# Rotary pair exchange by SBUF-to-SBUF DMAs, and small VectorE work handed to GpSimd and ScalarE, in a delta-rule attention and mixture-of-experts kernel

## The reference

```python
# attention block: 16 heads of 64
q, k, v = [silu(causal_dwconv(x @ W, cw, cb)) for W in (Wq, Wk, Wv)]     # 4 taps
q, k = rope(q), rope(k)                    # pairs (even, odd) are rotated by position
q, k = q * rsqrt(sum(q*q) + eps), k * rsqrt(sum(k*k) + eps)
beta  = sigmoid(x @ bw + bb)
alpha = exp(-exp(A_log) * softplus(x @ gkw + gkb + dt_bias))
for t in range(T):                         # delta rule, one state S per head
    o[t] = q[t] @ S + D * sum(q[t]*k[t]) * v[t]
    S = alpha[t] * (S - beta[t] * outer(k[t], k[t] @ S)) + beta[t] * outer(k[t], v[t])
on = o * rsqrt(mean(o*o) + eps) * onorm_w
y  = ((x @ Wg) * silu(on)) @ Wo
# second block: layernorm, 16 heads of 8 with softmax, then 8 experts of 512, the top 2 weighted
```

## Time and profile before

| | before |
|---|---|
| median of three runs | 5533.0 us |
| the profiled execution's own time | 5533.59 us |
| its span, first to last instruction | 5531.7 us |
| TensorE matmuls (PE) busy | 4792.2 us, 87% |
| weight loads (PEld) busy | 3609.5 us, 65% |
| VectorE (DVE) busy | 4623.1 us, 84% |
| ScalarE (ACT) busy | 3445.0 us, 62% |
| GpSimd (POOL) busy | 2085.5 us, 38% |
| mean granted TensorE clock | 0.843 of full speed |
| HBM read, written | 148.02 MB, 4.19 MB |

### The profile page before, as it was taken

The page is one execution under the profiler, slowest core; times in us unless marked ns, Lnnn a source line. Parts: engine busy times, 40 slices in busy tenths (PEclk is TensorE's granted clock), DMA queues, the critical chain, the costliest instruction groups (busy, mean ns, idle before and its releaser), DMA issues.

```text
span 5531.7 us, 111231 instructions
## 1 busy us (share of the span) xinstructions
PE 4792.2 (87%) x40448; PEld 3609.5 (65%) x40448; DVE 4623.1 (84%) x11457; ACT 3445.0 (62%) x6166; POOL 2085.5 (38%) x1485
## 2 busy tenths in 40 slices
PE   4688889988889898889898899888899888899986
PEld 2466667666667666667666677666677666677665
DVE  6888898888888888988888988888988888988852
ACT  3456666656666656766666666566666666666653
POOL 3443333443343442343443344433434433334420
PEclk7778898888888888988888888878988888888878
DMA  1001111011111011111111111111111011111011
GB/s 59 10 11 34 43 43 34 28 32 37 43 43 34 24 32 41 43 33 32 33 33 42 43 33 32 32 34 43 43 34 32 32 34 43 43 34 32 31 34 56
DMA packets 214453, 197.13 MB, mean 36 GB/s; under 512 B 13848, under 2 KB 176416, under 8 KB 209696
## 3 DMA queue, kind: packets, MB, share of 16 engines
q1 hardware_dynamic: 213920, 190.01, 11.1%
HBM read 148.02 MB, written 4.19 MB: 28 GB/s over the span
## 4 chain that ended last, share of the span: by engine, by line
DVE 52%; PE 38%; issue 8%; ACT 1%; SPq 0%; DMA 0%; POOL 0%; DVEq 0%; POOLq 0%; ACTq 0%
PE bank L984 36%; DVE acc L1390 10%; DVE tmpb L1556 6%; DVE NP L1526 6%; DVE Gam L1559 5%; DVE mx L1653 3%; DVE Gam L1512 3%; DVE moe L1738 2%; PE bank L988 2%; DVE QK L1671 1%; DVE QK L1479 1%; DVE Gam L1563 1%; DVE rot L1475 1%; DVE ms L1603 1%; DVE Kt L1543 1%
## 5 line engine op out<-in xcount | busy, mean ns | idle before, releaser
L1390 DVE SCALAR_TENSOR_TENSOR acc<-bank,conv_w,acc 128x255 f32<-128x255 f32 (+2 forms) x2304 | 925.1, 470 | 27.3 <-ACT acc L791 26.4
L717 POOL TENSOR_TENSOR sq<-acc 128x256 f32<-128x256 f32 x256 | 191.2, 747 | 1734.5 <-ACT acc L797 1722.3
L984 PE MATMUL bank<-QK 64*128 64x256 f32 (+1 forms) x4096 | 603.3, 352 | 211.8 <-DVE mx L1653 97.7
L984 PE MATMUL bank<-W,h 128*128 128x128 f32 x4096 | 579.7, 302 | 190.1 <-issue 103.3
L984 PEld LDWEIGHTS bank<-W,h 128*128 128x128 f32 x4096 | 551.7, 215 | 237.1 <-issue 129.6
L984 PE MATMUL bank<-mT,W 128*128 128x256 f32 x2048 | 626.4, 447 | 60.3 <-issue 39.7
L984 PEld LDWEIGHTS bank<-QK 64*128 64x128 f32 (+1 forms) x4096 | 288.6, 142 | 523.7 <-issue 346.0
L966 ACT ACTIVATE h<-bank,b 128x256 f32<-128x256 f32 x1024 | 416.7, 479 | 288.6 <-PE bank L984 286.7
L984 PEld LDWEIGHTS bank<-mT,W 128*128 128x128 f32 x2048 | 420.9, 220 | 219.2 <-issue 155.3
L729 POOL TENSOR_TENSOR rot<-rot,sin 128x512 f32<-128x512 f32 x256 | 337.3, 1317 | 450.8 <-DVE rot L1475 450.8
L1559 DVE TENSOR_TENSOR Gam<-Gam,tmpb 128x31 f32<-128x31 f32 (+15 forms) x992 | 448.1, 452 | 34.1
(11 more groups left out here) (226 smaller groups left out, 10275.4 us busy)
## 6 DMA issues: line engine op xcount, KB each, us to landing
W<-in_W SPq DMA_DIRECT2D x512, 256.0 KB, 3.2
QK<-QK SPq DMA_DIRECT2D x32, 1024.0 KB, 5.1
xin<-in_x SPq DMA_DIRECT2D x32, 128.0 KB, 4.7
x<-in_x SPq DMA_DIRECT2D x32, 128.0 KB, 2.1
xnG<-xnT SPq DMA_DIRECT2D x32, 128.0 KB, 1.9
out<-moe SPq DMA_DIRECT2D x32, 128.0 KB, 1.9
NP<-in_c_alpha_sel SPq DMA_DIRECT2D x1, 1024.0 KB, 5.4
Wqkv<-in_Wq SPq DMA_DIRECT2D x1, 512.0 KB, 6.1
```

What stands on the lines that cost most here:

```text
L984: return mm(out_, lhsT, rhs, start=first, stop=last)
L1390: v.scalar_tensor_tensor(acc[:, n % 2, m, j:T], ps[:, m, 0:T - j], conv_w[:, kind, c, PAD - j:KT - j], acc[:, n % 2, m, j:T], ALU.mult, AL ...
```

## The change

The result is the same function. Eight things are changed:

1. The even and odd partitions of `acc` are exchanged by two DMAs per chunk (128 KB each, 64 partitions of 2 KB) issued by SyncE, instead of a stream shuffle.
2. The addition of the rotation runs on GpSimd (`rope`, semaphore `p_QK` for `v_QK`).
3. The gate polynomial runs on GpSimd as 18 instructions (`poly`) instead of 12 on VectorE; a factor 2 went into `neg_A`.
4. The split of the maxima runs on GpSimd as 6 instructions instead of 5 on VectorE.
5. The split of `alpha` and of `fqk`: the casts and copies from PSUM run on ScalarE, and GpSimd takes the last part of `fqk` (`part2`).
6. The factor 1/64 of the mean square is taken by ScalarE's square, so a VectorE instruction per chunk goes.
7. `xnG` waits for all users of its old content, and `mx` for its reader.
8. `ORDER` and `BANK` are other tables.

```diff
-        dots:7@1 rstd:0@0 xs:0@3 sin:6@1 root:1@2 norm:0@2 norm:1@2 cos:7@1 nrm:0@1 sin:7@1 frstd:0@2 X:0@1 frstd:1@2
+        cos:0@0 vscale:0@1 dots:0@0 maxes:0@2 sin:0@0 dots:1@0 rope:0@0 cos:1@0 vscale:1@1 poly:0@0 sin:1@0 dots:2@0
...
+        solve:16@1 max:11@2 max:12@2 expert:5@3 max:13@2 max:14@2 max:15@2 fv:0@2 solve:17@1 mrow:0@2 solve:18@1
...
+            def swapped(k, n):
+                sp.wait_ge(a_silu.sem, a_silu.at(k, n + 1))
+                if begun(k, n - 1):
+                    sp.wait_ge(p_QK.sem, p_QK.at(k, n - 1))
+                for q in range(2):
+                    sp.dma_start(rot[q::2, n % 2], acc[1 - q::2, n % 2]).then_inc(rot_in[n % 2][q].sem, 16)
...
             def by_sin(k, c):
-                pool.wait_ge(v_rot.sem, v_rot.at(k, c + 1))
+                for q in range(2):
+                    pool.wait_ge(rot_in[c % 2][q].sem, rot_in[c % 2][q].at(k, 16 * (c // 2 + 1)))
...
+            def turned(k, c):
+                pool.wait_ge(p_rope.sem, p_rope.at(k, 2 * c + 2))
+                g.tensor_tensor(chunk(c), chunk(c), by_token(rot[:, c % 2]), ALU.add).then_inc(p_QK.sem, 1)
...
+            def gate(i, n):
+                pool.wait_ge(v_gate.sem, v_gate.at(i, 8))
+                g.tensor_tensor(lp2[:], lp[:], lp[:], ALU.mult).then_inc(p_gate.sem, 1)
+                pool.wait_ge(p_gate.sem, p_gate.at(i, 1))
+                g.tensor_scalar(lpp[:], lp2[:], 1.0 / 15, 1.0 / 13, ALU.mult, ALU.add).then_inc(p_gate.sem, 1)
+                for m, d in enumerate((11, 9, 7, 5, 3, 1)):
+                    pool.wait_ge(p_gate.sem, p_gate.at(i, 2 + 2 * m))
+                    g.tensor_tensor(lpp[:], lpp[:], lp2[:], ALU.mult).then_inc(p_gate.sem, 1)
+                    pool.wait_ge(p_gate.sem, p_gate.at(i, 3 + 2 * m))
+                    g.tensor_scalar(lpp[:], lpp[:], 1.0 / d, None, ALU.add).then_inc(p_gate.sem, 1)
...
+            def last_part(j, n):
+                pool.wait_ge(a_part.sem, a_part.at(j, 2))
+                g.tensor_tensor(part[:, 2], prest[:], part[:, 1], ALU.subtract).then_inc(p_part.sem, 1)
+
+            def max_parts(j, n):
+                pool.wait_ge(v_mx.sem, v_mx.at(j, FH))
+                if prev(j) is not None:
+                    pool.wait_ge(v_mrow.sem, v_mrow.at(prev(j), NC // 2))
+                g.tensor_scalar(mrest[:], mx[:], -1.0, None, ALU.mult).then_inc(p_mp.sem, 1)
...
             def gate_alpha(k, n):
-                act.wait_ge(v_gate.sem, v_gate.at(k, 20))
+                act.wait_ge(p_gate.sem, p_gate.at(k, 18))
...
+            def alpha_parts(i, n):
+                if n == 0:
...
+                    s.copy(al1[:], a_t).then_inc(a_al.sem, 1)
+                    s.copy(alpha3[0:H, :, 2:GW], a_t[:, :, 1:P]).then_inc(a_al.sem, 1)
+                else:
+                    act.wait_ge(v_alpha.sem, v_alpha.at(i, 1))
+                    s.copy(al2[:], alr[:]).then_inc(a_al.sem, 1)
+                    s.copy(alpha3[32:32 + H, :, 2:GW], alr[:, :, 1:P]).then_inc(a_al.sem, 1)
```

More of the change, by code:

```diff
@@ new lines @@
+        Dv:1@2 cos:5@1 xs:0@3 QSadd:0@2 root:0@2 QSadd:1@2 dots:6@1 sin:5@1 dots:7@1 norm:0@2 rope:4@1 rstd:0@0 root:1@2
+        norm:1@2 rope:5@1 cos:6@1 sin:6@1 cos:7@1 rope:6@1 frstd:0@2 sin:7@1 rope:7@1 frstd:1@2 part2:0@2 X:0@1 nrm:0@1
+        cos:0@0 vscale:0@1 dots:0@0 maxes:0@2 sin:0@0 dots:1@0 rope:0@0 cos:1@0 vscale:1@1 poly:0@0 sin:1@0 dots:2@0
+        cos:2@0 dots:3@0 rope:1@0 sin:2@0 cos:3@0 Dv:0@1 rope:2@0 frstd:2@2 sin:3@0 cos:4@0 R1:0@1 dots:4@0 R1:1@1
+        rope:3@0 sin:4@0 dots:5@0""",
@@ L435, in program @@
         a_siluV = signal("a_siluV", 4)
-        v_rot = signal("v_rot", NC)
+        rot_in = [[Signal(sem(f"rot_in_{m}_{q}"), 8 * NC) for q in range(2)] for m in range(2)]
         p_sq = signal("p_sq", NC)
@@ L734, in _ @@
                 "root": root, "norm": normalise, "frstd": root_ln, "xs": two_x, "vscale": scale_values, "dots": dots,
-                "cos": by_cos, "sin": by_sin})
+                "cos": by_cos, "sin": by_sin, "rope": turned, "poly": gate, "part2": last_part,
+                "maxes": max_parts})
         @block.scalar
@@ L1747, in _ @@
                 "ms": mean_square, "v": taps_v, "y": gated, "x1": first_sum, "fstat": stat, "fshift": shift_of,
-                "fqk": parts, "fv": values_f, "max": maxima, "maxes": max_parts, "mrow": less_max, "ctx": context,
+                "fqk": parts, "fv": values_f, "max": maxima, "mrow": less_max, "ctx": context,
                 "x2": second_sum, "router": router, "choice": choice, "wT": weights, "moe": first_moe,
```

287 lines of the change are left out of this document (136 added, 151 removed).

## The result

The changed kernel takes 5750.8 us (median of 4 runs, 5727.4 to 5789.8), the kernel before in the same comparison 5535.4 us. The ratio is 1.039, interval 1.0317 to 1.0463: it is slower by 3.9%, where 5290 us and a range of 5090 to 5540 had been forecast. The profiled execution took 5773.6 us, 240 us more than that of before. Ratios in this document leave out runs that took over 1.5% more than the fastest of their kernel, which are one of eight of `early_parts_dve` and two of the four of `early_fill_gaps` (5419.1, 5464.4, 5508.5 and 5513.1 us).

The account below looks back on a forecast made before the run. VectorE was taken to bound a turn's first stretch, TensorE its second: 97.8 + 1.6 - 2 + 2 = 99.4 us, plus 57.6, makes 157.0 against 164.6; 7.6 less, times 32, gives 5533 - 243 = 5290 us, range 5090 to 5540.

Parts of the forecast that it names:

- The first stretch: From a batch's `alpha:0` to its closed solve, bound by VectorE: 117.2 us a turn to become 99.4.
- the port: GpSimd products slow VectorE's solve steps at the shared SBUF port, 6.1 us a turn; 2 us of it gained.
- Coupling: First stretch: more waits between VectorE and TensorE, the latter 89% busy instead of 83%; 2 us a turn allowed.
- maxes: Maxima's split before `mrow`: six dependent GpSimd instructions and TensorE, not fully covered; VectorE waits 1.6 us a turn.
- What leaves VectorE's first stretch: Shuffles, additions, small groups and work moved behind the close leave VectorE there: 19.4 of 117.2 us a turn.
- SyncE's queue: 16 more DMAs a turn, `expert:6` behind the exchanges of chunks 2 to 5; counted at nothing, bound 2 us.
- The 20 us of cover from chunk to chunk: Between `silu` and `sin`: two buffers and some 20 us hide the exchange's extra 1.2 us, so nothing was counted.
- Second stretch: Closed solve to next batch's `alpha:0`, TensorE full: 10.2 us of moved work added, 47.4 to 57.6 us a turn.
- Small GpSimd instructions: Arithmetic on 32 elements, in polynomial and maxima's split: 0.29 us each, so the polynomial just fits ahead of `top`.
- One turn as the base: The change was priced on one profiled turn of 164.6 us and counted 32 times, once a batch.
- The slower one: Rival: small GpSimd instructions cost 0.7 us, so polynomial and maxima's split come late; 5570 to 5600 us, chance 0.14.
- TensorE alone bounds: Rival: with VectorE relieved, TensorE fills a turn of 151 us; 435 us gained, 5100 us, chance 0.22.

Follow-up runs that it names:

- early_parts_dve: The changed kernel with the edit, and the splits of `fqk` and of the maxima back on VectorE; 5591.5 us, ratio 1.0095 to the kernel before.
- early_fill_gaps: The changed kernel with the edit, and 12 products a turn that nothing reads added before four waits of TensorE; 5486.5 us, ratio 0.982.
- early_less_up: The changed kernel with the edit, the last quarter of the experts' first product left out; 5652.8 us, ratio 1.0216.
- the fillers: Runs with products that nothing reads added before TensorE's waits; 12 a turn in the changed kernel, its queue untouched, give 5546.1 us, ratio 1.0036.
- early_fill_more: The changed kernel with the edit, the products of early_fill_gaps, three more among the joins and 8 or so elsewhere a turn; 5416.2 us, ratio 0.9803.
- the edit: The changed kernel with only SyncE's order edited: exchange of chunk 6 first, chunk 7 behind `xnG`, `expert:6` ahead of chunks 2 to 5; 5604.3 us, ratio 1.0115.

## Why the prediction was wrong

The reading of before was right, and so was most of the count of work. What failed is the step that turned VectorE's load into time. The first stretch was forecast at 99.4 us and measures 120.3. Of the 20.9 us between, 13.2 are waits of VectorE beyond what was allowed, and 7.6 are busy time that was counted as gone (19.4 and 2 for the port) and wasn't.

- **Coupling: the step that failed most.** "TensorE has about 87 us left in this stretch (below) of 97.8, 89% where it was 83%. I allow 2 us for more waits between the two." VectorE's idle time in the stretch rose from 5.8 to 22.6 us a turn, where this term and `maxes` allowed 3.6 together; 17.5 us of it are waits for TensorE (before 3.1). TensorE lost 49 records there (691 to 643 on average), some 8 us of work at the prices of before, and was busy just as long, 99.1 us, at a clock of 0.86 for 0.92. A load of 87 us had been priced at the clock that it had while VectorE held the stretch at 117 us and TensorE's gaps lay elsewhere. `early_less_up` and the fillers show that the clock answers to the gaps, in the direction opposite to load. The 8.5 us that VectorE still waits in `early_fill_more`, at a higher clock than before the change, show that even then 2 us would have been too few.
- **What leaves VectorE's first stretch: counted right, cashed wrong.** 19.4 us and 2 for the port were forecast. Counting each instruction only where none before it still ran, some 19.7 us of busy time went, as forecast, but 5.8 us came back on instructions that took longer, so the busy time fell by 13.8 us, from 111.5 to 97.7. The prediction had also given a sign for it: VectorE's busy time in all was to fall to near 4070 us, and it is 4250.7.
- **The port: wrong sign.** 2 us of the 6.1 lost were forecast to come back. The solve's two lines did lose 1.0 us less a turn (842.6 us in 32 batches against 875.0). But of the 5.8 us that came back, 4.6 are on steps ahead of the solve, by the same count: `ms` went from 0.17 to 2.08 us a turn, the first half of `y` from 1.16 to 2.66, and the two `fshift` from 0.14 to 1.34 together. In the turn from 2858.0, `ms` and the first `fshift` end within 0.04 us of a GpSimd product, and that half of `y` ends 1.07 us behind one. GpSimd's product and `ms`, of 16 elements a partition:

```profile
2861.32 2.35 POOL L709 TENSOR_TENSOR Gam<-Gam,onorm 128x1024 f32<-128x1024 f32 x1
...
2861.61 2.10 DVE L1658 SCALAR_TENSOR_TENSOR ms<-sk,ms 128x16 f32<-128x16 f32 x1
```

- **SyncE's queue: the uncosted wait.** "Bounds: nothing, or 2 us", and only `expert:6` was looked at. The order of this queue cost 146 us of the run, 4.6 us a turn. The traced wait is chunk 6's behind `expert:0`; the edit also moved chunk 7 and `expert:6`, and the share of each wasn't tried. The order table showed where chunk 6 stands. The 20 us of cover from chunk to chunk, on which the exchange was counted at nothing, isn't there at the turn's start. The named sign, `sin` waiting long for the exchange, appeared.
- **Second stretch: 57.6 forecast, 54.7 measured.** The base was 2.3 us too short (47.4 in the turn read, 49.7 on average), and the increase 5.0 us where 10.2 were counted. The 49 records that came in take about 9 us at the prices of the changed kernel, but TensorE's busy time rose only from 49.7 to 52.4 us, at a clock of 0.81 for 0.69.
- **Small GpSimd instructions: right.** Forecast 0.29 us, measured:

```profile
L761 POOL TENSOR_SCALAR lpp<-lpp 128x32 f32<-128x32 f32 x192 | 55.7, 290 | 16.8
...
L759 POOL TENSOR_TENSOR lpp<-lpp,lp 128x32 f32<-128x32 f32 x192 | 48.3, 252 | 16.0
```

  The exponential behind the polynomial ran at 2978.53, ahead of the first `top`, as counted. But the wait for the maxima's split was 3.7 us a turn, not 1.6.
- **One turn as the base.** 164.6 us was one of the shorter turns; the mean is 167.0. It moves the sum little, but in the kernel before the second stretch already went with the clock from turn to turn, from 46.5 us at 0.74 to 52.7 at 0.64. That was a sign that TensorE's clock counts.
- **The rivals.** The slower one named the price of small instructions, which was right as forecast. "TensorE alone bounds" had the engine but the wrong sign: it was worked out at a constant clock and made the kernel faster.

Not settled: how the waits of 8.5 us that remain in the best version come about, and whether fillers would help the new order with the old code, where they weren't run. Which gap costs most of the clock wasn't tried singly either.
